# Local attention with 1/sum multiplied into the exponentials, ahead of their transposes

## What is computed

```
q, k, v = heads(shift_token(x) @ wqkv)            # 8 heads of 64, windows of 128 tokens
q, k = rotary(l2norm(q) * qs), rotary(l2norm(k) * ks)
sim = 8 * q @ k.T                                 # each window sees itself and the window before: 128 x 256
sim[i < j or i > j + 128 or j == -1] = -max
attn = softmax(sim, axis=-1)
out = attn @ v
x = x + out @ wo
h = layernorm(shift_token(x)) * lg + lb
x = x + (a * gelu(g)) @ w2 + b2                   # a, g = split(h @ w1 + b1), 2 x 682
```

## Time and profile before

| | |
|---|---|
| median of 3 runs | 2962.12 us (2961.7 to 2962.24) |
| the profiled execution | 2961.06 us, its span 2959.0 us |
| PE busy | 2839.2 us (96% of the span) |
| ACT busy | 2366.8 us (80%) |
| DVE busy | 2208.8 us (75%) |
| POOL busy | 1643.3 us (56%) |
| chain of work that ended last | 90% PE |
| mean granted clock of PE | 0.984 of full speed |

### The profile page before, as it was taken

The page is one execution under the profiler, slowest core; times in us unless marked ns, Lnnn a source line. Parts: engine busy times, 40 slices in busy tenths (PEclk is TensorE's granted clock), DMA queues, the critical chain, the costliest instruction groups (busy, mean ns, idle before and its releaser), DMA issues.

```text
span 2959.0 us, 67980 instructions
## 1 busy us (share of the span) xinstructions
PE 2839.2 (96%) x23460; PEld 2582.5 (87%) x23460; DVE 2208.8 (75%) x6587; ACT 2366.8 (80%) x5429; POOL 1643.3 (56%) x1652
## 2 busy tenths in 40 slices
PE   7999938999999999999999999999999999999987
PEld 6878826799999989999999999999999999999987
DVE  3979967778777777787777777777777777777763
ACT  4989946788888888888888888888888888888873
POOL 2323225666666666666666555666666666666643
PEclk9999968999999999999999999999999999999999
DMA  3152111111111111111110212111111111111000
GB/s 97 62 180 76 39 57 38 34 41 40 34 41 36 38 36 40 41 40 38 36 41 27 68 41 88 33 34 33 33 34 33 34 34 34 33 34 32 29 19 30
DMA packets 139624, 132.16 MB, mean 45 GB/s; under 512 B 16402, under 2 KB 134932, under 8 KB 138260
## 3 DMA queue, kind: packets, MB, share of 16 engines
q1 hardware_dynamic: 139284, 127.82, 14.2%
HBM read 77.33 MB, written 42.05 MB: 40 GB/s over the span
## 4 chain that ended last, share of the span: by engine, by line
PE 90%; DVE 3%; ACT 2%; POOL 2%; issue 2%; SPq 1%; DMA 1%; POOLq 0%; DVEq 0%; ACTq 0%
PE ps L385 50%; PE ps L359 10%; PE ps L469 8%; PE ps L455 7%; PE ps L443 7%; PE ps L428 4%; PE ps L479 2%; PE ps L405 1%; PE ps L497 1%; ACT Sm L730 1%; POOL rs L1200 1%; PE ps L346 1%; PE ps L534 1%; PE ps L533 0%; SPq L1383 0%
## 5 line engine op out<-in xcount | busy, mean ns | idle before, releaser
L730 ACT ACTIVATE Sm<-Sm,nb,sc 128x256 f32<-128x256 f32 (+1 forms) x1024 | 597.6, 588 | 2.2 <-DVE nb L1061 1.4
L1054 DVE CUSTOM_DVE_ANT_0 Sm<-ps,mask 128x256 f32<-128x256 f32 (+1 forms) x1024 | 368.3, 415 | 79.5 <-PE ps L443 77.3
L1127 DVE SCALAR_TENSOR_TENSOR Gl<-ps,vecs,Gl 128x256 f32<-128x256 f32 (+1 forms) x384 | 173.3, 479 | 317.5 <-ACT Gl L774 161.0
L385 PE MATMUL ps<-zTh,W1h 128*128 128x256 f32 (+1 forms) x1408 | 405.3, 288 | 0.0
L385 PE MATMUL ps<-zTl,W1h 128*128 128x256 f32 (+1 forms) x1408 | 397.4, 282 | 0.0
L385 PE MATMUL ps<-zTh,W1l 128*128 128x256 f32 (+1 forms) x1408 | 393.1, 279 | 0.0
L1200 POOL TENSOR_TENSOR rs<-rs,mhalf 128x16 f32<-128x16 f32 x128 | 372.3, 2909 | 0.0
L710 ACT ACTIVATE sq<-ps 128x512 f32<-128x512 f32 x256 | 152.5, 596 | 254.6 <-PE ps L385 254.1
L1291 POOL TENSOR_TENSOR uTl<-Gl,uTh 128x512 fp32r<-128x512 f32 (+1 forms) x192 | 211.0, 1105 | 254.6 <-ACT uTh L784 202.0
L385 PE MATMUL ps<-WQh,hTh 128*128 128x512 f32 x768 | 341.9, 445 | 2.8 <-DVE hTl L1011 2.8
L385 PE MATMUL ps<-WQl,hTh 128*128 128x512 f32 x768 | 305.0, 397 | 0.0
(11 more groups left out here) (188 smaller groups left out, 8982.4 us busy)
## 6 DMA issues: line engine op xcount, KB each, us to landing
tb<-tab SPq DMA_DIRECT2D x128, 128.0 KB, 2.3
xc<-x SPq DMA_DIRECT2D x32, 256.0 KB, 3.1
rwkv_scratch<-rw SPq DMA_DIRECT2D x32, 256.0 KB, 2.6
rk<-rwkv_scratch SPq DMA_DIRECT2D x64, 128.0 KB, 2.3
xin<-x SPq DMA_DIRECT2D x64, 128.0 KB, 2.2
x_scratch<-x SPq DMA_DIRECT2D x64, 128.0 KB, 1.7
y_scratch<-os SPq DMA_DIRECT2D x64, 128.0 KB, 4.1
y<-y_scratch SPq DMA_DIRECT2D x64, 128.0 KB, 4.0
```

The source lines that it names most:

```text
L385: ins = pe.matmul(dst, L(a), R(b), start=start and i == 0, stop=stop and i == 2)
L730: act.activation(Sm[:, h, c0:c1_], Sm[:, h, c0:c1_], ACT.Exp, bias=nb[:, h:h + 1], scale=sc[:, n % 4, h:h + 1], accum_out=sm[:, n % 2, h:h ...
L1054: dve.tensor_tensor_reduce(Sm[:, h, c0:c1_], PS[:, bank["scores", n, q, h % 2], (h // 2 % 2) * 256 + c0:(h // 2 % 2) * 256 + c1_], mask[:, ...
L1127: dve.scalar_tensor_tensor(out=Gl[0:v, j % 4, :], in0=s, scalar=V("b1a", 6 * l + j, 0, v), in1=gl, op0=ALU.add, op1=ALU.mult).then_inc(S[" ...
```

## The change

The exponentials themselves are normalised before they are transposed. `p_sums(n, q)` (DVE) makes four reciprocals for each half. `p_norm` multiplies four heads of Sm, 128 x 1024 values, by their reciprocals in place: heads 0 to 3 on POOL (semaphore pn0), heads 4 to 7 on DVE (pn1). `turn_p` now waits for pn0 (j = 0, 1) or pn1 (j = 2, 3) where it waited for the exponentials. `spread`, `turn_r`, `rT_out` and `o_norm`, the tiles rob and oF and the PSUM bank of rT are gone. `oT_hi` and `oT_lo` read the product with v straight from its PSUM bank, which is free only after `oT_lo`. On ACT `oT_hi` moves from late in the step to just behind `exp(t-5, 1)`; on DVE `oT_lo` moves from behind `masked_max` to just behind `x2_out`. The first four exponentials of a window wait for the reciprocals of the half that used the same sums before.

```diff
@@ psum_order2
     if live(6):
-        yield "rT", t - 6
         yield "pv", t - 6
@@ read_out
             if what == "pv":
-                return S["on"], n + 1
+                return S["oTl"], n + 1
@@ tensor_program, turn_p
-                w.wait_ge(S["ex"], 8 * n + 2 * j + 2)
+                if j < 2:
+                    w.wait_ge(S["pn0"], n + 1)
+                else:
+                    w.wait_ge(S["pn1"], n + 1)
@@ tensor_program, order
                 if live(6):
-                    turn_r(t - 6)
                     pv(t - 6, 0)
@@ scalar_program
             def oT_hi(n):
-                w.wait_ge(S["on"], n + 1)
+                w.wait_ge(S["p6"], 2 * n + 2)
                 w.wait_ge(S["p8"], n)
-                act.activation(flat(oT[0][:, :, :]), flat(oF[:, :, :]), ACT.Copy).then_inc(S["oTh"], 1)
+                act.activation(flat(oT[0][:, :, :]), PS[:, bank["pv", n], :], ACT.Copy).then_inc(S["oTh"], 1)
@@ scalar_program, order
-                if live(6):
-                    rT_out(t - 6)
                 if live(5):
                     exp(t - 5, 1)
+                if live(6):
+                    oT_hi(t - 6)
@@ vector_program
+            def p_sums(n, q):
+                r = slice(4 * q, 4 * q + 4)
+                w.wait_ge(S["ex"], 8 * n + 4 * q + 4)
...
+                dve.reciprocal(ro[:, r], sm[:, n % 2, r]).then_inc(S["ro"], 1)
+
+            def p_norm(n):
+                c0, c1_ = cols(n)
+                w.wait_ge(S["ro"], 2 * n + 2)
+                dve.tensor_tensor(Sm[:, 4:8, c0:c1_], Sm[:, 4:8, c0:c1_],
+                                  ro[:, 4:8].unsqueeze(2).broadcast_to([128, 4, c1_ - c0]), ALU.mult).then_inc(S["pn1"], 1)
@@ vector_program, order
                     pre_y(t - 1)
+                if live(5):
+                    p_sums(t - 5, 0)
                 if live(9):
                     z_norm(t - 9)
                 if live(8):
                     z_stats(t - 8)
-                if live(6):
-                    o_norm(t - 6)
+                if live(5):
+                    p_sums(t - 5, 1)
+                    p_norm(t - 5)
                 if live(7):
                     x2_out(t - 7)
                     zero_h2(t - 7)
+                if live(6):
+                    oT_lo(t - 6)
@@ gpsimd_program
-            def spread(n):
-                w.wait_ge(S["ro"], n + 1)
-                w.wait_ge(S["p7"], n)
-                pool.tensor_copy(rob[:, :, :], ro[:, :].unsqueeze(2).broadcast_to([128, 8, 64])).then_inc(S["rob"], 1)
+            def p_norm(n):
+                c0, c1_ = cols(n)
+                w.wait_ge(S["ro"], 2 * n + 1)
+                pool.tensor_tensor(Sm[:, 0:4, c0:c1_], Sm[:, 0:4, c0:c1_],
+                                   ro[:, 0:4].unsqueeze(2).broadcast_to([128, 4, c1_ - c0]), ALU.mult).then_inc(S["pn0"], 1)
```

More of the change, by code:

```diff
@@ L260, in build @@
         ro = sb("ro", [8])
-        rob = sb("rob", [8, 64])
-        oF = sb("oF", [4, 128])
         oT = pair("oT", [4, 128])
@@ L297, in read_out @@
                 return S["x2"], n + 1
-            if what == "rT":
-                return S["rT"], n + 1
             if what == "zT":
@@ L472, in pv @@
                 ins.then_inc(S["p6"], 1)
[L474 to L481, removed]
             def wo_mm(n):
@@ L727, in exp @@
                 w.wait_ge(S["nb"], 2 * n + q + 1)
-                w.wait_ge(S["ro"], n - 1)
+                w.wait_ge(S["ro"], 2 * (n - 2) + q + 1)
                 for h in range(4 * q, 4 * q + 4):
@@ L811, in scalar_program @@
                     gelu((t - 11) // 2, 2)
-                if live(6):
-                    oT_hi(t - 6)
                 if live(2):
@@ L1062, in masked_max @@
                                          op1=ALU.mult).then_inc(S["nb"], 1)
[L1064 to L1071, removed]
-                dve.tensor_tensor(flat(oF[:, :, :]), PS[:, bank["pv", n], :], flat(oF[:, :, :]),
-                                  ALU.mult).then_inc(S["on"], 1)
+            def p_sums(n, q):
+                r = slice(4 * q, 4 * q + 4)
+                w.wait_ge(S["ex"], 8 * n + 4 * q + 4)
+                if q:
+                    w.wait_ge(S["pn1"], n)
+                else:
+                    w.wait_ge(S["pn0"], n)
+                dve.reciprocal(ro[:, r], sm[:, n % 2, r]).then_inc(S["ro"], 1)
[4 more added lines that the diff above has]
+                                  ro[:, 4:8].unsqueeze(2).broadcast_to([128, 4, c1_ - c0]), ALU.mult).then_inc(S["pn1"], 1)
             def oT_lo(n):
@@ L1077, in oT_lo @@
                 w.wait_ge(S["p8"], n)
-                dve.tensor_tensor(flat(oT[1][:, :, :]), flat(oF[:, :, :]), flat(oT[0][:, :, :]).bitcast(F32),
+                dve.tensor_tensor(flat(oT[1][:, :, :]), PS[:, bank["pv", n], :], flat(oT[0][:, :, :]).bitcast(F32),
                                   ALU.subtract).then_inc(S["oTl"], 1)
@@ L1172, in vector_program @@
                     u_tail((t - 11) // 2)
-                if live(6):
-                    oT_lo(t - 6)
-                if live(5):
-                    o_sums(t - 5)
                 if live(2):
@@ L1344, in gpsimd_program @@
                     nT_lo(t)
-                if live(5):
-                    spread(t - 5)
                 if live(2):
```

## The result

The changed kernel takes 3254.5 us (median of 4 runs, 3250.3 to 3258.8) against 2962.0 (2961.7 to 2962.2) before: ratio 1.0988, 95% interval 1.0969 to 1.1007. It is slower by 292 us, or 9.9%. Predicted were 3207, and 3095 to 3290.

A forecast was written before the change was run, and what follows sets the result against it. PE was taken to bound the kernel (90% of the span). The profiled 2961.1 us, plus 168 for new waits less removed transposes, plus 78 for the clock, gave 3207 us; range 3095 to 3290.

The forecast's parts named there:

- The bound and the wait: PE bounds the kernel; its new wait for POOL's Sm before the transposes costs full length, near 236 us in all.
- POOL's multiply: Heads 0 to 3, 128 x 1024 with a broadcast operand: 1.95 us, from a measured half-size row doubled, less some start-up.
- Down step, layer one: First transposes: pre_y stands ahead of the reciprocals on DVE, so PE waits 3.5 us for POOL's multiply.
- Down step, layer two: First transposes: zT_lo stands ahead of the multiply in POOL's queue, so PE waits 3.0 us.
- Up step, layer one: First transposes: reciprocals follow pre_y on DVE, then POOL's multiply; PE waits 1.45 us.
- Up step, layer two: First transposes: the multiply ends before PE needs it, a new wait of 0.
- The filling steps: Six windows before the MLP works (steps 5 to 10), where PE has idle time: -3 us.
- Transposes: The removed PE transposes of rob: 0.53 us in each of 128 steps, 68 us gained in all.
- The clock: PE's clock falls to half behind 8 of 10 down-step gaps, 1.6 us each: +78 us, bounds 0 and 144.
- Heads 4 to 7 on DVE cost nothing: DVE's multiply of the second half is done before PE's later transposes need it, covered by 1.7 us.
- The rival of contention: POOL and DVE hold each other up; POOL's multiply takes 2.4 us instead of 1.95: 3275 us, chance 0.15.
- The other side: The multiply's wait is hidden and the gain from the removed transposes stays: 2893 us, chance 0.06.

The follow-up runs named there:

- e1: Changed kernel without its two multiplies, output not normalised, transposes waiting for the exponentials alone: 2918.9 us.
- e2: Changed kernel with matmuls that nobody reads put on PE ahead of the first transposes, sized to its wait, none in the filling steps: 3163.0 us.
- e3: Changed kernel with the first two transpose groups moved later, behind the w2 product or the middle MLP part: 3136.9 us.
- e5: Changed kernel with late transposes, POOL's multiply at the end of the step before, ahead of zT_lo, and DVE's first reciprocals ahead of pre_y: 3197.5 us.
- e6: Changed kernel with both multiplies on DVE, none on POOL, and the first reciprocals ahead of pre_y: 3061.5 us.
- e8: Changed kernel without multiplying the exponentials; each transpose becomes a matmul with a diagonal of 1/sum made by DVE: 3161.2 us.

## Why the prediction was right

- **The bound and the wait.** Right. PE waited for POOL's Sm, and for almost nothing else that is new. The total agrees better than its parts: 251 us were measured and 236 predicted, but only 220 of them lie in the steps for which the 236 were worked out. The other 31 lie in the filling steps, which were put at no wait. That the two errors have opposite signs is luck.
- **POOL's multiply**: 1.95 predicted, 1.90 measured. The choice of the broadcast row, doubled, was right. The estimate of 2.25 us, worked out from the Trainium skill's GPSIMD Engine Reference, section 3.1, is too high for this form. The total that the prediction gave by it was also a little off: 0.3 us more in each of 88 waits is 26 us, so 3233 and not 3240.
- **Down step, layer one**: 3.5 predicted, 3.59 in nearly all of them (95 us in 27 waits). **Down step, layer two**: 3.0 predicted, 2.70 in most (90 us in 34). **Up step, layer one**: 1.45 predicted, 1.22 in most (34 us in 27). **Up step, layer two**: 0 predicted, 0.9 us in all. The errors are of both signs and small.
- **The filling steps** were counted as -3 us, transposes gone and no wait. This is the term that failed: six waits of 4.0 to 7.6 us stand there, and the filling lost 23.5 us. PE is not the bound there (busy for 60.8 of the 100 us from 400 to 500 us before the change), and the prediction read no rows of these steps.
- **Transposes**: -68 predicted. No run shows this gain by itself; e1 shows 43, with 25 us of new waits for oTl that the changed kernel does not have.
- **The clock**: 78 predicted, from a fall behind 8 of 10 down steps at 1.6 us each. The share was right, 52 of 61. The price was too small: 17 of the 53 stretches were 6.8 us instead of 3.4. Half of the 239 us at half clock, 119, bounds the cost. e2 measures 91. The remainder of the spans gives 3253 - 2959 - 24 (filling) - 220 - 8 (waits) + 65 (transposes) = 107, or 84 if the waits are counted at the weight load, which is held first and longer: 238.5 us for POOL's Sm and 13.0 for Br instead of 220.4 and 8.0. So 84 to 107, with 91 by experiment.
- **Heads 4 to 7 on DVE cost nothing**: right for the changed kernel (0.9 us of wait). But the cover was thinner than it seemed. It holds because PE is late: e3 and e5 took that away and paid 32 and 130 us.
- **The rival of contention**: its mechanism is there, its price is not. It foresaw POOL's multiply lengthened to 2.4; that stayed at 1.9 and DVE's z_norm was held instead, where it delayed nobody that PE waits for.
- **The gap of 47 us** between 3207 and 3254 (49 to the profiled run): the filling steps +27, the waits behind them -15, the small waits for Br +8, the clock and what is not placed +29, of which e2 gives 13 to the clock.

The other side was never near: even with the multiply a step early, the best order found lost 48 us. Whether some other order beats the 2962 of the kernel before is neither shown nor excluded.

## What to carry to other kernels

When PE is the bound and its order is written by hand, work taken off PE is a gain only as long as what takes its place is not upstream of PE in the same step: 68 us of transposes were exchanged for a link of 1.9 us in front of PE, for which it waited in 96 of 128 windows. Work out the steps that fill the pipeline too: they were 5% of the windows and lost 24 us. Price a link by the queue it stands in, not by the engine's busy share: find what is released last, what stands ahead of it, and what short instruction stands behind it. Before improving a wait, ask which wait is second; here each mend at one queue uncovered the next one.

## What the runs showed of the hardware

- A multiply on POOL (1.90 us, changed kernel) holds a DVE tensor_scalar from and to SBUF (128x128, 0.34 us) that starts just behind it until it ends (1.92; median of 128 1.917, and 0.341 in e6, without the work on POOL). The reverse was seen too: POOL's power of 128x16, 2.91 us, takes 3.52 when it starts inside a multiply of DVE.
- The multiply of 128x1024 with a broadcast operand takes 1.22 us on DVE and 1.90 on POOL (medians of the changed kernel).
- A PE that is given useless work in its waits (e2) keeps a granted clock of 1.00 there and ends 91 us earlier than one that is left idle, whose clock was 0.96 from 1760 to 3140 us.
- A float32 matmul of 128x128 with a diagonal takes two instructions of 0.28 us (e8, x4032), the transpose of the same tile one (changed kernel, x2016).
